# Three edits around the start of a fused attention and routed feed-forward kernel: counts of tokens in FP32R, products of the identity in iteration 0, and statistics in two groups

## The reference

```python
xn = _layernorm(x, axis=-1)
x = x + _L0_attn_ref(xn, ...) + _L0_ffn_ref(xn, ...)
# in _L0_ffn_ref, N = 4096 tokens, H = 512, E = 8
logits = x_flat @ W_router
probs = jax.nn.sigmoid(logits)
topk_probs, topk_idx = jax.lax.top_k(probs, TOPK)
topk_probs = topk_probs / (jnp.sum(topk_probs, axis=-1, keepdims=True) + 1e-06)
combine = jnp.zeros((N, E), dtype=x.dtype).at[jnp.arange(N)[:, None], topk_idx].add(topk_probs)
out = sq_relu(x_flat @ W_sh_up) @ W_sh_down
for e in range(E):
    h = sq_relu(x_flat @ W_up[e])
    out = out + combine[:, e:e + 1] * (h @ W_down[e])
```

## Time and profile before

| | |
|---|---|
| median of 3 runs | 477.09 us |
| lowest and highest | 472.55 and 478.1 us |
| profiled execution | 479.72 us |
| its span | 477.9 us |
| mean granted PE clock in it | 0.96 |
| busy share PE / DVE / ACT / POOL | 92% / 73% / 62% / 32% |

### The profile page before, as it was taken

How to read it: one execution, slowest core, us unless ns; L and a number is a source line. 1 busy time by engine, 2 the same in 40 slices (tenths; PEclk the granted TensorE clock), 3 DMA queues, 4 the chain that set the end, 5 groups by cost and what they waited for, 6 DMA issues and landing times.

```text
span 477.9 us, 12359 instructions
## 1 busy us (share of the span) xinstructions
PE 437.6 (92%) x4354; PEld 347.4 (73%) x4355; DVE 350.0 (73%) x691; ACT 295.3 (62%) x515; POOL 153.5 (32%) x175
## 2 busy tenths in 40 slices
PE   8889678789999999959999999999999999999992
PEld 8877446556666666649999999999976666666661
DVE  8967886877888888845665665665639999998632
ACT  1444445457778777735666666656657876787660
POOL 5270000436556665600000000000015554555563
PEclk9989868979999999968999999999999999999998
DMA  8482201223235434343555545545113433342222
GB/s 228 158 353 78 74 9 67 80 91 117 96 103 167 140 129 145 111 121 104 162 138 145 160 137 147 156 143 154 45 41 106 124 109 94 102 135 69 80 56 67
DMA packets 64177, 56.61 MB, mean 118 GB/s; under 512 B 6658, under 2 KB 56324, under 8 KB 63620
## 3 DMA queue, kind: packets, MB, share of 16 engines
q1 hardware_dynamic: 59364, 42.49, 29.1%
q0 software_dynamic: 4096, 8.40, 6.0%
q10 hardware_dynamic: 672, 5.11, 2.5%
HBM read 26.61 MB, written 16.52 MB: 90 GB/s over the span
## 4 chain that ended last, share of the span: by engine, by line
PE 72%; DVE 17%; issue 4%; DMA 2%; ACT 1%; POOL 1%; SPq 1%; POOLq 0%; DVEq 0%; ACTq 0%
PE pbank L1305 15%; PE obank L1169 10%; PE sbank L1194 10%; DVE maxes L903 7%; PE fbank L1132 4%; PE fbank L1024 3%; PE fbank L1025 3%; PE fbank L1026 3%; PE tbank L1024 3%; PE tbank L1026 2%; PE tbank L1025 2%; PE sbank L1297 2%; PE pbank L1024 2%; PE wbank L1148 2%; PE wbank L1141 2%
## 5 line engine op out<-in xcount | busy, mean ns | idle before, releaser
L903 DVE TENSOR_REDUCE maxes<-sbank 128x4 f32<-128x1024 f32 x128 | 156.6, 1224 | 41.9 <-PE sbank L1194 38.9
L658 ACT ACTIVATE probs<-tbank 128x1024 f32<-128x1024 f32 x128 | 130.9, 1023 | 77.3 <-PE tbank L1199 76.9
L495 POOL DMA_INDIRECT gathered<-results,place_of x64 | 60.9, 952 | 203.3 <-DMA results<-gathered 153.0
L486 POOL DMA_INDIRECT slots<-X,place_of x64 | 61.9, 968 | 73.9 <-PE tbank L1199 68.6
L1194 PE MATMUL sbank<-k_bands,q_bands 31*128 31x256 f32 x512 | 66.0, 335 | 19.1 <-DVE maxes L903 16.7
L1194 PEld LDWEIGHTS sbank<-k_bands,q_bands 31*128 31x128 f32 x512 | 40.0, 189 | 56.6 <-DVE maxes L903 43.5
L1305 PE MATMUL pbank<-down_w,probs 128*128 x624 | 76.5, 276 | 0.6 <-ACT gathered L704 0.6
L1305 PEld LDWEIGHTS pbank<-down_w,probs 128*128 128x128 f32 x624 | 73.2, 193 | 0.8 <-issue 0.8
L1169 PE MATMUL obank<-probs,v_ones 128*32 128x256 f32 x1024 | 71.1, 396 | 0.0
L1199 PE MATMUL tbank<-q_bands,k_bands 32*128 32x256 f32 x512 | 65.7, 335 | 0.8 <-ACT probs L658 0.8
L995 DVE TENSOR_TENSOR block_lo<-block_w,block_hi 128x512 fp32r<-128x512 f32 x39 | 27.0, 692 | 47.8 <-ACT block_hi L689 47.7
(11 more groups left out here) (167 smaller groups left out, 833.2 us busy)
## 6 DMA issues: line engine op xcount, KB each, us to landing
block_w<-in_w_up SPq DMA_DIRECT2D x39, 256.0 KB, 2.6
results<-gathered SPq DMA_DIRECT2D x39, 128.0 KB, 2.0
q_bands<-part_hi SPq DMA_DIRECT2D x32, 128.0 KB
k_bands<-part_hi SPq DMA_DIRECT2D x32, 128.0 KB
slots<-q_bands ACTq DMA_DIRECT2D x1, 4096.0 KB, 11.5
gathered<-slots SPq DMA_DIRECT2D x20, 128.0 KB, 2.1
relu_T<-slots SPq DMA_DIRECT2D x19, 128.0 KB, 2.1
q_bands<-part_lo SPq DMA_DIRECT2D x16, 128.0 KB
```

What stands on the lines that cost most here:

```text
L486: pool.indirect_dma_start(out=slots, out_offset=bass.IndirectOffsetOnAxis(ap=place_of[:, k, t:t + 1], axis=0), in_=X[:, t, :], in_offset=N ...
L495: pool.indirect_dma_start(out=gathered[:, c % 2, k * TT + t, :], out_offset=None, in_=results, in_offset=bass.IndirectOffsetOnAxis(ap=plac ...
L658: nc.scalar.activation(probs[:, j % 4, :], tbank[:], ACT.Exp, scale=SCALE).then_inc(exps_ready, 1)
L903: nc.vector.tensor_reduce(maxes[:, g // 2, :, 2 * pair:2 * pair + 2, g % 2].rearrange("p t q -> p q t"), sbank[:].rearrange("p (q t k) -> ...
```

## The change

Three edits, which touch PE, DVE, ACT and POOL.

1. `later`, `sel`, `tile_sums` and `chosen` become tensors of FP32R with places of their own, and `same_once` is an FP32R copy of `same`. So the two products of `sum_tiles` and the five of `count` are FP32R products.
2. `FILL` gets 3, 3, 3, 2 and 4 products of the identity at the end of slots (0, 3) to (0, 7). They are written to fbank, behind a wait for ACT's reading of the logits.
3. The statistics of tiles 12 to 31 are split. `prepare(1)` takes tiles 12 to 19, with inverse roots in (-2, 5); those of tiles 20 to 31 stand in slot (-2, 7), with roots on ACT in (-1, 0) behind two chunks' standardising and inverse roots in (-1, 2).

```diff
+STATISTICS = (-2, 7)
...
-FILL = {(-2, 3): 22, (-1, 0): 16}
+FILL = {(-2, 3): 22, (-1, 0): 16, (0, 3): 3, (0, 4): 3, (0, 5): 3, (0, 6): 2, (0, 7): 4}
...
-        later = sb("later", [P, 2, TILES * E])
+        later = sb("later", [P, 2, TILES * E], F32R)
         same = sb("same", [P, E])
+        same_once = sb("same_once", [P, E], F32R)
+
+        sel = sb("sel", [P, 2, P], F32R)
+        chosen = sb("chosen", [P, TILES, E], F32R)
+        tile_sums = sb("tile_sums", [P, 2, P], F32R)
...
+            nc.gpsimd.tensor_copy(same_once[:], same[:]).then_inc(later_ready, 1)
...
-            pool.wait_ge(rstd_ready, 3)
+            pool.wait_ge(rstd_ready, 4)
...
                 if c == 3:
-                    roots(3, 3 * CHUNK, TILES)
+                    roots(3, 3 * CHUNK, 5 * CHUNK)
                     act.wait_ge(rstd_ready, 3)
                     standardise(3)
                     standardise(4)
+                    roots(4, 5 * CHUNK, TILES)
                 high_part(c)
...
                 if c == 1:
                     inverse_roots(2, CHUNK, 3 * CHUNK)
-                    for k in range(2, 5):
-                        dve.wait_ge(tokens_loaded[k], 16)
-                    statistics(3 * CHUNK, TILES)
+                    dve.wait_ge(tokens_loaded[2], 16)
+                    statistics(3 * CHUNK, 5 * CHUNK)
                 else:
                     low_part(c - 1)
                 if c == 2:
-                    inverse_roots(3, 3 * CHUNK, TILES)
+                    inverse_roots(3, 3 * CHUNK, 5 * CHUNK)
+                if c == 4:
+                    inverse_roots(4, 5 * CHUNK, TILES)
...
                         prepare(TURN[b, j])
+                    if (b, j) == STATISTICS:
+                        for k in range(3, 5):
+                            dve.wait_ge(tokens_loaded[k], 16)
+                        statistics(5 * CHUNK, TILES)
...
-            def fill(n):
+            def fill(n, to=obank):
 
                 for _ in range(n):
-                    nc.tensor.matmul(obank[:, 0:P], ident[:], ident[:], start=True, stop=True)
+                    nc.tensor.matmul(to[:, 0:P], ident[:], ident[:], start=True, stop=True)
...
-                    nc.tensor.matmul(fbank[:, n:n + E], tile_sums[:, h, :], same[:], start=h == 0, stop=h == 1)
+                    nc.tensor.matmul(fbank[:, n:n + E], tile_sums[:, h, :], same_once[:], start=h == 0, stop=h == 1)
...
-                    fill(FILL.get((b, j), 0))
+                    if (b, j) == (0, 3):
+
+                        pe.wait_ge(exp_logits_ready, 1)
+                    fill(FILL.get((b, j), 0), obank if b < 0 else fbank)
```

More of the change, by code:

```diff
@@ L159, in build @@
         rows = probs[0:1].rearrange("p a b -> p (a b)")
-        sel = gathered[:, 0, 0:2, :]
         rawsh = out_raw[:].rearrange("p n t -> p (n t)")
@@ L166, in build @@
         ys = gathered[:, 0]
-        tile_sums = gathered[:, 0, 2:4, :]
         counts = down_w[:, LATE:].rearrange("p e c d -> p (e c d)")[:, 6 * TILES * E:7 * TILES * E + E]
@@ L458, in selectors @@
             def selectors():
-                nc.gpsimd.memset(sel, 1.0).then_inc(selectors_ready, 1)
+                nc.gpsimd.memset(sel[:].bitcast(F32), 1.0).then_inc(selectors_ready, 1)
                 pool.wait_ge(selectors_ready, 1)
-                nc.gpsimd.affine_select(out=sel[:, 0, :], in_=sel[:, 0, :], compare_op=ALU.is_gt, fill=0.0, base=0,
+                nc.gpsimd.affine_select(out=sel[:, 0, :], in_=sel[:, 0, :].bitcast(F32), compare_op=ALU.is_gt, fill=0.0, base=0,
                                         pattern=[[1, P]], channel_multiplier=-1).then_inc(selectors_ready, 1)
@@ L512, in _ @@
                 pool.wait_ge(later_ready, 2 * h + 1)
-                nc.gpsimd.affine_select(out=later[:, h, 0:TILES * E], in_=later[:, h, 0:TILES * E], compare_op=ALU.is_gt, fill=0.0,
+                nc.gpsimd.affine_select(out=later[:, h, 0:TILES * E], in_=later[:, h, 0:TILES * E].bitcast(F32), compare_op=ALU.is_gt, fill=0.0,
                                         base=-P * h, pattern=[[1, TILES * E]], channel_multiplier=-1).then_inc(later_ready, 1)
+            nc.gpsimd.tensor_copy(same_once[:], same[:]).then_inc(later_ready, 1)
             pool.wait_ge(shared_up_loaded, 16)
             split(rawsh)
-            pool.wait_ge(rstd_ready, 3)
+            pool.wait_ge(rstd_ready, 4)
             for c in range(CHUNKS - POOLED, CHUNKS):
@@ L603, in routing @@
                     act.wait_ge(tile_sums_done, 1)
-                    nc.scalar.activation(tile_sums.rearrange("p h d -> p (h d)"), fbank[:, 0:2 * P], ACT.Copy).then_inc(tile_sums_kept, 1)
+                    nc.scalar.activation(tile_sums[:].rearrange("p h d -> p (h d)"), fbank[:, 0:2 * P], ACT.Copy).then_inc(tile_sums_kept, 1)
                 if (b, j) == (1, 1):
@@ L848, in choose @@
                     first(1)
-                    nc.vector.tensor_tensor(table(5), table(1), table(2), ALU.add).then_inc(chosen_ready, 1)
+                    nc.vector.tensor_tensor(chosen[:], table(1), table(2), ALU.add).then_inc(chosen_ready, 1)
                 if j == 7:
@@ L1065, in _ @@
             pe.wait_ge(wqk_split, 1)
-            chosen = table(5).rearrange("p t e -> p (t e)")
+            all_chosen = chosen[:].rearrange("p t e -> p (t e)")
             def sum_tiles():
@@ L1073, in sum_tiles @@
                 for h in range(2):
-                    ins = nc.tensor.matmul(fbank[:, h * P:h * P + P], chosen[:, h * P:h * P + P], sel[:, 1, :], start=True, stop=True)
+                    ins = nc.tensor.matmul(fbank[:, h * P:h * P + P], all_chosen[:, h * P:h * P + P], sel[:, 1, :], start=True, stop=True)
                 ins.then_inc(tile_sums_done, 1)
@@ L1079, in count @@
                 pe.wait_ge(tile_sums_kept, 1)
-                pe.wait_ge(later_ready, 4)
+                pe.wait_ge(later_ready, 5)
                 n = TILES * E
-                nc.tensor.matmul(fbank[:, 0:n], sel[:, 0, :], chosen, start=True, stop=False)
+                nc.tensor.matmul(fbank[:, 0:n], sel[:, 0, :], all_chosen, start=True, stop=False)
                 for h in range(2):
@@ L1085, in count @@
                 for h in range(2):
-                    ins = nc.tensor.matmul(fbank[:, n:n + E], tile_sums[:, h, :], same[:], start=h == 0, stop=h == 1)
+                    ins = nc.tensor.matmul(fbank[:, n:n + E], tile_sums[:, h, :], same_once[:], start=h == 0, stop=h == 1)
                 ins.then_inc(counted, 1)
```

## The result

| | kernel before | changed kernel |
|---|---|---|
| median | 476.34 us (22 runs) | 478.66 us (22 runs) |
| lowest and highest | 472.55 to 479.55 | 476.33 to 481.15 |
| profiled execution / its span | 479.72 / 477.9 us | 480.91 / 479.1 us |
| mean granted PE clock in it | 0.960 | 0.967 |

The ratio of the changed kernel to the one before is 1.0058, with a 95% interval of 1.0039 to 1.0076: within 2%, and slower by 1.9 to 3.6 us. The forecast was 477.3 us in a range of 473.0 to 481.5, on a kernel before of 477.09 us by three runs; by 22 runs its median is 476.34.

A forecast was written before the change was run, and what follows sets the result against it. Bounds: DVE at 17 to 26 us, PE at 32 to 50, DVE at 50 to 69. Counts -2.6, identity +0.2, statistics +2.6 gave +0.2 on 479.7, 479.9 us; less 2.6, median 477.3, range 473.0 to 481.5.

The forecast's parts named there:

- even as the likeliest: Case for the whole kernel: all terms as summed, median 477.3 us, within 475.5 to 479; chance 0.50.
- the statistics win, slower: Case: clock falls at 26 to 33 us, identity products run at half clock; +2.9 us, 480.0; chance 0.18.
- The statistics: Iteration -1: second statistics ahead of slot 0's row maxima make them late; +2.6 us, bounds +0.6 and +3.8.
- POOL hidden: POOL's twelve standardisations start later but stay hidden, about 3 us to spare; rival of a collision, +6 to +9, chance 0.03.
- Products of the identity: 15 products in iteration 0's slots 3 to 7 lie in PE's waits; +0.2 us, bounds 0 and +1.4.
- the cover is DVE's 17.6 us: At 50 to 69 us DVE is busy for 17.6 us, so the products of the identity cost next to nothing.
- Counts in one pass: sum_tiles and count as FP32R products: -2.3 us at half clock, -3.5 at full clock, taken as -2.6.
- Handed on unchanged: From iteration 1 on engines wait only for each other, so gain or loss by then reaches the end unchanged.
- a way to be wrong: Wrong if DVE's second statistics lie beside idle time, or clock falls behind iteration 1 differ by over 3 us.
- half clock is what it shows there now: At sum_tiles and count the trace shows half clock, so -2.3 us was weighed more than -3.5.

The follow-up runs named there:

- e1: Changed kernel with only the statistics split: counts in FP32, no products of the identity in iteration 0; 479.84 us, ratio 1.0111.
- e5: Changed kernel with the statistics of tiles 20 to 31 behind the row maxima of slot 0 and their inverse roots in (-1, 3); 475.50 us, ratio 0.9986.
- e6: Changed kernel with 26 instead of 16 products of the identity in slot (-1, 0); 477.97 us, ratio 1.0029.
- e11: e5 with 9 instead of 3 products of the identity in slot (0, 3); 474.59 us, ratio 0.9960.
- e7: e2 without the three products of the identity in slot (0, 4); 473.98 us, ratio 0.9957.
- e9: e5 without the three products of the identity in slot (0, 4); 474.47 us, ratio 0.9971.
- e12: e10 with all five tensors of the counts in FP32 as in the kernel before; 474.18 us, ratio 0.9977.
- e3: e2 without the products of the identity in iteration 0, so only the counts in FP32R; 477.36 us, ratio 1.0014.
- e4: Kernel before with only the 15 products of the identity in iteration 0 added; 475.14 us, ratio 0.9997.
- e2: Changed kernel with the statistics in one block of twenty again; 475.32 us, ratio 1.0010.
- e10: e2 with 9 instead of 3 products of the identity in slot (0, 3); 475.19 us, ratio 0.9978.
- e8: Kernel before, unchanged, run once more for a second trace; span ends at 473.4 us against 477.9 in the first trace.

## Why the prediction was right, and where it was not

**Sign and size.** The forecast was +0.2 us on the kernel before and even as the likeliest; measured is +1.9 to +3.6. The absolute time lay in the range, and even within the 475.5 to 479 of the likeliest case, but not for that case's reasons. That is luck in part: the range was wide against the change, and the terms for the counts and for the identity did not come true. Of the cases the one called "the statistics win, slower" (+2.9) comes closest, and it had 0.18.

**The statistics: the mechanism right, step for step.** By the times in the sum DVE was to stand for 1.2 us (19.4 to 20.6) and for 0.9 (21.3 to 22.2); it stands for 1.17 and 0.84. scores(-1, 1) and project_values(0) come +2.0 and +2.3 us late at full clock (e1), as reckoned. The clock falls behind the new wait in the changed kernel's trace, which brings it to +4.5; I had taken +2.6 with a bound of +3.8. What the text left open, whether it is the place or the splitting, e5 has settled: the place, for all but 0.4 us. (e6, with the clock full there, comes to +2.3 at the maxima of slot 2 as e1 does.)

**POOL hidden: right for the changed kernel.** 0.79 us a tile as before, and nothing waits. The reserve is small, though: in e11 PE waits 1.17 us for POOL.

**Products of the identity: sized too low.** "I take 0.2" for an edit whose bound was +1.4. With three products in each of the slots (0, 3) and (0, 4) the clock had already fallen at slot (0, 4) in four of five traces (not in e5), and in these the distance from (0, 4) to (0, 5) is 1.2 to 1.4 us above that of the first trace of the kernel before, iteration 0 as a whole 0.8 to 0.9 us. e7, which leaves out just these, has the lowest ratio, though not clear of e9 to e12. The argument that the cover is DVE's 17.6 us was right for the others alone: in slot (0, 4) PE's own wait was 0.41 us, and this row should have been taken at its word. The price of one product at half clock, 0.6 us taken over from sum_tiles, was on the other hand too high: three take 1.48 us, 0.49 each.

**Counts in one pass: the step that failed.** "I take -2.6", between -2.3 at half clock and -3.5 at full clock. PE's part was nearly as short as forecast: at half clock 0.69 us for sum_tiles and 1.06 for count in e3, where 0.44 and 0.88 were reckoned. But e3's distance is 0.7 us shorter, not 2.3; the clock came back later there (about 78.4 instead of 74.2 us), which I had charged with 0.6 us only. The -3.5 of full clock is what the pair of traces shows (9.5 to 6.1), but e4 has 3.1 of it with the counts in FP32: it is the clock and not the one pass. At the same clock the traces give the one pass 0.7 us (e2 against e4) to 1.1 (e9 against e1). At full clock the counts are no longer what comes last: PE waits 1.06 us for ACT's copy ahead of up(0, 0) in e2, and 0.48 in e4. In the timed runs both edits together are worth +0.1% (-0.2 to +0.4, e2), and e12 against e10 shows no worth of the one pass. So the sum should have been about 0 for these two, +2.3 to +3 for the statistics.

**Handed on unchanged: not in this pair.** The prediction takes it that what is lost by iteration 1 reaches the end as it is. In the two traces 3.3 us have become 1.2 at the end, as the clock's fall behind 206 us is shorter in the changed kernel. Such a shorter fall (3.5 to 7 us instead of about 10) stands in five of the seven traces that also have a fall near 100 us, and in none of the others; behind the last row maxima these five take 272.7 to 273.3 us, the nine others 274.8 to 275.2. So about 2 of the 2.9 us that a fall near 100 us costs come back in them. Why the two go together isn't shown. The prediction had named falls behind iteration 1 that differ by more than 3 us as a way to be wrong; the one behind 206 us differs by about that.

**One trace is not the kernel.** The prediction drew "half clock is what it shows there now" from a single execution with a mean clock of 0.960, and scaled the result to the median by subtracting 2.6 us. The timed runs have 0.970, and e8 shows the same kernel with 1.5 us less in the same distance. The 3.5 us that the change gains there in this pair of traces are therefore more than it gains on the average. What the average kernel before spends there stays open: two traces of it don't make a mean.

## What to carry to other kernels

Where a block is split to let its first part go earlier, look at what the second part is put ahead of, and at whether the consumer of the first part is ready: here it was not (ACT was at its transfers), and the maxima behind the second part were on the path. Fill an engine's wait only up to the length of that wait at the clock that it has there. The longest wait is the place to try first: with nine products in it the clock stayed full there in three traces of three, with three in one of seven, though the timed runs don't prove a gain over e2 or e5. Where a product's duration depends on the granted clock, don't price an edit from one trace; take a second one of the same kernel, or the mean clock of the timed runs, before the sum is made.

## What the runs showed of the hardware that was not expected

The products at the start of the kernel can take as long as at half clock for up to 14 us, and the column of the granted clock doesn't show it. Twelve recorded products of the identity near 8 us, in the first trace of the kernel before and in that of the changed kernel:

```profile
7.59 1.60 PE L1052 MATMUL obank<-ident 128*128 128x128 f32 x12
```

```profile
8.55 2.93 PE L1065 MATMUL obank<-ident 128*128 128x128 f32 x12
```

1.60 us against 2.93, that is 0.13 and 0.24 us a record, where 0.12 is that of full clock (3.84 us for 32) and 0.25 that of half clock (1.48 for 6). The windows of both print 1.00 there. With products as slow as that the mark of the statistics comes later: 17.0 to 17.2 us in nine of the twelve traces of experiments and in the first of the kernel before, 18.4 to 19.8 in three of them and in the changed kernel. How much of such a late start reaches the end isn't shown: e10 has the latest mark, 19.83, and the shortest span of all, 472.2 us. The fall around 100 us stands in 7 of the 14 traces, and from (2, 0) to (3, 0) it costs 2.8 to 3.0 us in six of them and 1.4 in e1. These are the largest differences seen between traces; whether they make up the 5 to 8 us by which timed runs of one kernel lie apart stays open.

Less work on PE was no gain by itself in e3: with the counts alone in one pass the median clock of the timed runs was 0.960 instead of 0.970, and with 15 more products of the identity (e4) it was 0.976, with times within 0.2% of the kernel before by the ratios. The Trainium skill (TensorE: Matmul & The Clock Gate, What's actually happening) says that the default state is throttled and activity releases the throttle; e3 and e4 agree. Between e10 and e12, which differ by the one pass alone, there is no such difference: 0.979 and 0.980.
